# Running sums of a state-space scan: from additions on GpSimd to accumulating DMAs, with the closing of a segment spread over more pairs and the experts leading by 12

## The chip, the cores and the metric

The kernel runs on one core of a Trainium2 chip, as one program. The metric is the device time of one launch, in microseconds (us). The kernel before took 618.33 us (median of 3 runs, 615.45 to 619.60).

## The reference

Two layers work on x of shape (1, 2048, 128), each behind a modulated layer norm. The first has a decaying linear attention with a small feed-forward block, and then a mixture of 8 experts. The second has a selective state-space scan, and then a product in the frequency domain that is linear in its input. The change touches the scan and what follows it:

```python
# experts: hidden 512, the two best of 8 weigh the sum
h = gelu(einsum('te,ieh->tih', x, w1) + b1)
out = sum((einsum('tih,ihe->tie', h, w2) + b2) * weights[..., None], axis=1)
# scan over 2048 tokens: 256 channels, 16 states
dt = softplus(x[:, :, :64] @ W_dt.T + b_dt); Bm = x @ W_B.T; Cm = x @ W_C.T
dA = exp(dt_t[:, :, None] * A[None])
h = dA * h + (dt_t * xv_t)[:, :, None] * B_t[:, None, :]
y_t = einsum('bdn,bn->bd', h, C_t)          # the sum over the 16 states
y = (y * silu(z)) @ W_out.T
```

## The kernel before, in words

The tokens are cut into four segments of 512. The first 170 us or so hold the attention and its feed-forward block. After them comes one loop over "pairs of states": a pair p is two of the 16 states of a segment, so a segment has 8 pairs (NP) and there are 32 in all. The loop runs from p = -AHEAD to 31. In pass p every engine does its share of expert g = p + AHEAD (32 of them, 8 for each segment) and of pair p. With AHEAD = 13 the loop has 45 passes: 13 with an expert alone, 19 with an expert and a pair, 13 with a pair alone.

In one pass:

- PE: the expert's up products (L1204 to L1206, four quarters of three matmuls), its down products (L1216), and for each state one matmul that spreads the B row over all partitions into the bank pB (`row_b`, L1282).
- ACT: four GELUs (`hidden`, L958), then four exponentials `dA` for the next pair (`decays`, L970). It loads a table before either.
- DVE: for each state a product into PSUM (`products`, L733) and two scans (`scans`, L746, tile Hs, one half for each state of the pair), a small reduction of the last column (L750), and once a pass the sum of the expert's result into X (`moe_acc`, L717).
- POOL: for each state the product with the C row (`output`, L386), and, in the pairs below ALONE = 18, an addition to the segment's running sum (L392). The running sum lives in half of Zev. In the pairs from ALONE on, PE adds the products into the banks pY (`total`, L1298 and L1302).
- SP: loads the C rows of a pair, four pairs ahead (L327).

A table in `later_stages` puts the other work into passes, by the number k of the pair in its segment. An entry names a place in the pass: "A" and "B" stand on PE between the expert's products, "C" at its end, "mid" between the two states on DVE, "end" after them, "apply" at the end of ACT's pass. Closing a segment (its "tail") is: `gate` (the sum times silu(z), L490 on POOL or L757 on DVE), `project` (L1313 on PE, and L762 on DVE), the layer norm (`ln_stats`, `ln_apply`, `ln_turn`), `bias` (L456) and `fft` (L1321, L768). Preparing the next one (its "front") is: `ln_stats`, `ln_apply` (L820), `ln_turn` (L1014 and L834), and from k = 5 on the matmuls of `x_part` (L1257), `rows`, `dt_part` and `z_part`. On every engine the order of instructions is that of the program; semaphores make one engine wait for another.

## Time and profile before

| | us |
|---|---|
| median of 3 runs | 618.33 |
| the profiled execution | 618.62 |
| its span in the profile | 616.3 |
| PE busy | 494.2 (80%) |
| DVE busy | 429.7 (70%) |
| POOL busy | 373.5 (61%) |
| ACT busy | 360.7 (59%) |

The busy shares are means over stages that differ: no engine is busy all the time, and the shares alone don't say which of them sets the pace of a pass. The profiled execution took 2.3 us more than its span.

### The profile page before, as it was taken

To read this page: it belongs to the slowest core of one execution; us is meant where nothing else is said; L and a number is where in the kernel's file an instruction comes from. 1 tells how busy PE (TensorE), PEld (TensorE's weight loads), DVE (VectorE), ACT (ScalarE), POOL (GpSimd) and SP (SyncE) were. 2 spreads that over 40 slices of the span, in tenths; PEclk is the share of its full clock that TensorE was granted. 3 is DMA by queue.
4 is the path that set the end of the run, shared out by engine and by line. 5 is a ranking of instruction groups with operands and counts; after the bars stand their busy time and mean duration, and the time that the engine had idled before them with its cause. 6 is when DMAs were issued, how large, how long until landed. Compare 5 with 4: busy or idle time off the path is not lost.

```text
span 616.3 us, 6905 instructions
## 1 busy us (share of the span) xinstructions
PE 494.2 (80%) x2358; PEld 346.0 (56%) x2358; DVE 429.7 (70%) x723; ACT 360.7 (59%) x505; POOL 373.5 (61%) x234
## 2 busy tenths in 40 slices
PE   3878877679899999988879987969987678766663
PEld 3466555444678888667756766856766433233222
DVE  4757888964542441048997786988785996999961
ACT  0432442325675575689989985979985555734301
POOL 3225976847201111218999997999996767557541
PEclk9977998989999999999999988899988989889877
DMA  8600000000000000400202010112110112212000
GB/s 295 259 1 0 1 1 1 1 0 0 1 1 1 2 1 1 139 0 35 69 35 71 34 70 30 41 51 71 35 64 9 65 51 70 69 69 80 5 1 17
DMA packets 12562, 26.93 MB, mean 44 GB/s; under 512 B 1968, under 2 KB 7472, under 8 KB 12272
## 3 DMA queue, kind: packets, MB, share of 16 engines
q1 hardware_dynamic: 11952, 25.57, 11.9%
q10 hardware_dynamic: 576, 0.92, 0.4%
q8 instruction: 19, 0.31, 0.2%
q14 instruction: 15, 0.12, 0.1%
HBM read 25.31 MB, written 1.18 MB: 43 GB/s over the span
## 4 chain that ended last, share of the span: by engine, by line
DVE 34%; POOL 27%; PE 24%; issue 6%; ACT 6%; DMA 1%; ACTq 0%; POOLq 0%; DVEq 0%
POOL Zod L386 11%; POOL Zev L392 11%; DVE Hs L746 10%; DVE pCT L733 6%; PE pO L1216 5%; DVE S L641 5%; DVE pH L640 3%; PE pY L1076 1%; PE pY L1302 1%; PE pH L1204 1%; PE pH L1257 1%; ACT gel L958 1%; DMA S<-in_w_mod 1%; PE pY L1257 1%; PE pY L1313 1%
## 5 line engine op out<-in xcount | busy, mean ns | idle before, releaser
L1216 PEld LDWEIGHTS pO<-w_e,gel 128*128 128x128 f32 x1024 | 126.8, 198 | 17.9 <-issue 8.8
L1216 PE MATMUL pO<-w_e,gel 128*128 128x128 f32 x1024 | 129.0, 281 | 5.0 <-DVE X L717 4.7
L746 DVE TENSOR_TENSOR_SCAN Hs<-dA,HL,pCT 128x512 f32<-128x512 f32 x96 | 117.7, 1267 | 6.1 <-POOL Zod L386 4.5
L958 ACT ACTIVATE gel<-pH,b_e 128x512 f32<-128x512 f32 x128 | 86.0, 687 | 48.5 <-PE pH L1206 47.8
L970 ACT ACTIVATE dA<-dt,a_neg 128x512 f32<-128x512 f32 x128 | 81.9, 711 | 35.4 <-DVE Hs L746 35.2
L733 DVE TENSOR_TENSOR pCT<-u,pB 128x1024 f32<-128x1024 f32 x64 | 78.3, 1224 | 25.2 <-PE pB L1282 24.2
L386 POOL TENSOR_TENSOR Zod<-Hs,Crow 128x1024 f32<-128x1024 f32 x33 | 78.3, 2373 | 13.2 <-DVE Hs L746 11.6
L392 POOL TENSOR_TENSOR Zev<-Zev,Zod 128x1024 f32<-128x1024 f32 x33 | 79.9, 2422 | 2.6
L1204 PE MATMUL pH<-h2h,w_e1h 128*128 128x512 f32 x128 | 58.3, 456 | 20.4 <-ACT gel L958 19.1
L717 DVE SCALAR_TENSOR_TENSOR X<-pO,wts,X 128x128 f32<-128x128 f32 x128 | 35.8, 342 | 40.6 <-PE pO L1216 40.5
L386 POOL TENSOR_TENSOR Zev<-Hs,Crow 128x1024 f32<-128x1024 f32 x17 | 41.0, 2414 | 36.8 <-DVE Hs L746 33.3
L435 POOL TENSOR_TENSOR ZA<-Qsb,S 128x1024 f32<-128x1024 f32 x16 | 38.0, 2377 | 33.9 <-DVE S L641 32.6
L1282 PE MATMUL pB<-ST,sel 96*128 96x512 bf16 x64 | 25.7, 401 | 34.2 <-DVE pCT L733 34.0
L1206 PE MATMUL pH<-h2h,w_e1l 128*128 128x512 f32 x128 | 51.3, 401 | 0.0
L1205 PE MATMUL pH<-h2l,w_e1h 128*128 128x512 f32 x128 | 51.2, 400 | 0.0
L1204 PEld LDWEIGHTS pH<-h2h,w_e1h 128*128 128x128 f32 x128 | 24.2, 189 | 36.1 <-ACT gel L958 32.2
L386 POOL TENSOR_TENSOR ZS<-Hs,Crow 128x1024 f32<-128x1024 f32 x14 | 33.0, 2358 | 17.9 <-DVE Hs L746 17.9
L820 ACT ACTIVATE ln_x<-X,ln_nb,ln_rs 128x128 f32<-128x128 f32 x48 | 19.7, 481 | 34.2 <-POOL ln_nb L352 34.2
L746 DVE TENSOR_TENSOR_SCAN Hs<-dA,pCT 128x512 f32<-128x512 f32 x32 | 37.3, 1207 | 3.3 <-POOL Zod L386 2.6
L884 ACT COPY Qsb<-pCT 128x1024 f32<-128x1024 f32 x16 | 16.2, 1013 | 36.7 <-PE pCT L1092 36.7
L1282 PEld LDWEIGHTS pB<-ST,sel 96*128 96x128 bf16 x64 | 6.3, 98 | 53.0 <-DVE pCT L733 47.1
L1091 PE MATMUL pH<-qk_hi,pick 128*128 128x512 f32 x32 | 16.2, 507 | 22.2 <-DVE S L641 22.1
(223 smaller groups left out, 922.7 us busy)
## 6 DMA issues: line engine op xcount, KB each, us to landing
Crow<-c_rows SPq DMA_DIRECT2D x32, 512.0 KB, 3.7
w_e<-in_w_e SPq DMA_DIRECT2D x2, 2048.0 KB, 10.7
X<-in_x SPq DMA_DIRECT2D x4, 256.0 KB, 7.7
out<-h2T SPq DMA_DIRECT2D x4, 256.0 KB, 2.3
S<-in_w_mod ACTq DMA_DIRECT2D x2, 384.0 KB, 5.4
w_cx<-in_conv_row SPq DMA_DIRECT2D x1, 512.0 KB, 8.9
w_f<-in_w_f SPq DMA_DIRECT2D x2, 128.0 KB, 5.6
b_e<-in_b_e SPq DMA_DIRECT2D x1, 256.0 KB, 13.4
```

The source lines that it names most:

```text
L386: pool.tensor_tensor(Z, Hs[:, 2 * o:2 * o + 2, 0:w], Crow[:, 2 * (p % NCB) + o:2 * (p % NCB) + o + 1, 0:w].to_broadcast([P, ND, w]), ALU.m ...
L392: pool.tensor_tensor(acc_of(c), acc_of(c), Z, ALU.add).then_inc(s["mam_zs"], 1)
L435: pool.tensor_tensor(ZA[:, :, :], Qsb[:, 2 * (R % 2):2 * (R % 2) + 2, :], S[:, 2 * r:2 * r + 2, :], ALU.mult).then_inc(s["att_zo"], 1)
L717: ins = vec.scalar_tensor_tensor(Xj, pO[:, j * P:(j + 1) * P], wts[:, c, j * E + e:j * E + e + 1], Xj, ALU.mult, ALU.add)
L733: vec.tensor_tensor(pU[:, :, 0:w], half_of(u, c), pB[:, None, 0:w].to_broadcast([P, ND, w]), ALU.mult).then_inc(s["mam_ub"], 1)
L746: vec.tensor_tensor_scan(Hs[:, 2 * o + d, 0:w], dA[:, 4 * (p % 2) + 2 * o + d, 0:w], pU[:, d, 0:w], HL[:, d, n:n + 1] if c else 0.0, ALU.m ...
L958: nc.scalar.activation(gel[:, n % NG, 0:w], pH[n % 2][:, 0:w], ACT.Gelu_apprx_tanh, bias=b_e1[:, NK * e + k:NK * e + k + 1]).then_inc(s["m ...
L970: nc.scalar.activation(dA[:, 4 * (p % 2) + r, 0:WIDTHS[c]], half_of(dt, c)[:, r % 2, :], ACT.Exp, scale=a_neg[:, r % 2, n:n + 1]).then_inc ...
L1204: mm(pH[n % 2][:, 0:w], w_e1h[:, g % E, part], h2h[:, c, 0:w], start=True, stop=False)
L1205: mm(pH[n % 2][:, 0:w], w_e1h[:, g % E, part], h2l[:, c, 0:w], start=False, stop=False)
L1206: mm(pH[n % 2][:, 0:w], w_e1l[:, g % E, part], h2h[:, c, 0:w], start=False, stop=True).then_inc(s["moe_h"], 1)
L1216: ins = mm(pO[:, j * P:(j + 1) * P], gel[:, n % NG, j * P:(j + 1) * P], w_e2[:, NK * (g % E) + k, :], start=(k == 0 and j == 0), stop=(k = ...
```

## The change

There are four parts.

1. **Sums by DMA.** In pairs below ALONE the products of both states go to a whole tile (Zev for even pairs, ZS for odd ones), and one DMA issued by GpSimd adds that tile to `Acc` (128 x 2048 f32, 1 MB). The first pair of a segment writes its products straight into `Acc`. The additions of L392 go. Each DMA waits until the one before it has landed, and the products two pairs later wait for it too. `Acc` keeps the two states apart; `gate` adds its halves once.
2. **The closing is spread.** `gate` goes from the end of pass 0 to the middle of pass 1, `project` from 1 to 2, the sum into X and the statistics from the middle of pass 1 to the end of pass 2, `ln_turn` from place A of pass 3 to place C, with a tile h5T of its own.
3. **AHEAD = 12**, so ALONE = 20, and the loop has 12 passes with an expert alone, 20 with both, 12 with a pair alone.
4. **The preparation** starts (`ln_stats` of the front) in pass 4 and no longer in pass 3.

```diff
@@ -35,3 +35,3 @@
 NCB = 4
-AHEAD = 13
+AHEAD = 12
 HALO = TAPS - 1
@@ -160,3 +160,2 @@
         Zev = sb("Zev", [P, 2 * ND, TC])
-        Zod = sb("Zod", [P, ND, TC])
         ZS = sb("ZS", [P, 2 * ND, TC])
@@ -173,2 +172,4 @@
         HL = sb("HL", [P, ND, NS])
+        Acc = sb("Acc", [P, 2, 2 * ND, TC])
+        h5T = sb("h5T", [P, TC])
         outb = h2T[:, :].rearrange("p (j d) -> p j d", j=NJ)
@@ -213,2 +214,7 @@
 
+        def tail_bank(c):
+
+            return [(stage_bank(p, at)) for p, stages in later_stages() for at, stage, q, *_ in stages
+                    if stage == "project" and q == c][0]
+
         def totals(p):
@@ -221,10 +227,5 @@
 
-        def adds(m):
-
-            return m - m // NS
+        def sums(p):
 
-        def acc_of(c):
-
-            h = ND * ((c + 1) % 2)
-            return Zev[:, h:h + ND, 0:WIDTHS[c]]
+            return len([q for q in range(min(p + 1, ALONE)) if q % 2 == p % 2 and q % NP])
 
@@ -247,2 +248,3 @@
         mam_c = [sem(f"mam_c{i}") for i in range(NCB)]
+        mam_s = [sem(f"mam_s{i}") for i in range(2)]
         NSM, NAT, NFF, NMO, NMA = 6, 2, 2, 5, 10
@@ -263,7 +265,7 @@
                 if 0 <= tail:
-                    plan += [(0, "end", "gate", tail), (1, "A", "project", tail), (1, "mid", "ln_stats", tail),
-                             (2, "apply", "ln_apply", tail), (2, "end", "bias", tail), (3, "A", "ln_turn", tail, 2),
-                             (4, "A", "fft", tail)]
+                    plan += [(1, "mid", "gate", tail), (2, "A", "project", tail), (2, "end", "tail_x", tail),
+                             (2, "end", "ln_stats", tail), (3, "apply", "ln_apply", tail), (3, "C", "ln_turn", tail, 2),
+                             (3, "end", "bias", tail), (4, "A", "fft", tail)]
                 if 0 <= front < NL:
-                    plan += [(3, "mid", "ln_stats", front), (4, "apply", "ln_apply", front), (4, "C", "ln_turn", front, 1),
+                    plan += [(4, "mid", "ln_stats", front), (4, "apply", "ln_apply", front), (4, "C", "ln_turn", front, 1),
                              (5, "A", "x_part", front, 0), (5, "B", "rows", front), (6, "A", "x_part", front, 1),
@@ -281,4 +283,5 @@
             last = NL - 1
-            for stage in (("A", "total", NL * NP - 1), ("end", "gate", last), ("A", "project", last), ("end", "bias", last),
-                          ("mid", "ln_stats", last), ("apply", "ln_apply", last), ("A", "ln_turn", last, 2), ("A", "fft", last)):
+            for stage in (("A", "total", NL * NP - 1), ("end", "gate", last), ("A", "project", last), ("end", "tail_x", last),
+                          ("end", "bias", last), ("mid", "ln_stats", last), ("apply", "ln_apply", last),
+                          ("A", "ln_turn", last, 2), ("A", "fft", last)):
                 yield (NL * NP, [stage])
@@ -365,3 +368,3 @@
                 h = slice(2 * (p % 2), 2 * (p % 2) + 2)
-                first = k == 0 and o == 0
+                part = slice(2 * o, 2 * o + 2)
                 if alone(p):
@@ -370,8 +373,7 @@
                         pool.wait_ge(s["mam_y"], totals(p - 2))
-                    elif o == 0 and p % 2 == (c + 1) % 2:
-                        pool.wait_ge(s["mam_y"], 1)
-                    elif o == 0:
-                        pool.wait_ge(s["mam_y2"], 2 * c)
-                elif first:
-                    Z = acc_of(c)
+                    elif p == ALONE and o == 0:
+                        for q in (p - 2, p - 1):
+                            pool.wait_ge(mam_s[q % 2], 16 * sums(q))
+                elif k == 0:
+                    Z = Acc[:, c % 2, part, 0:w]
                     if c >= 2:
@@ -379,5 +381,5 @@
                 else:
-                    Z = Zod[:, :, 0:w]
-                    if adds(m - 1):
-                        pool.wait_ge(s["mam_zs"], adds(m - 1))
+                    Z = [Zev, ZS][p % 2][:, part, 0:w]
+                    if p >= 2 and o == 0 and sums(p - 2):
+                        pool.wait_ge(mam_s[p % 2], 16 * sums(p - 2))
                 if o == 0:
@@ -389,6 +391,13 @@
                 done["mam_z"] = m + 1
-                if not alone(p) and not first:
-                    pool.wait_ge(s["mam_z"], m + 1)
-                    pool.tensor_tensor(acc_of(c), acc_of(c), Z, ALU.add).then_inc(s["mam_zs"], 1)
-                    done["mam_zs"] = adds(m)
+
+            def add_up(p):
+
+                c, k = divmod(p, NP)
+                if alone(p) or k == 0:
+                    return
+                w = WIDTHS[c]
+                pool.wait_ge(s["mam_z"], 2 * p + 2)
+                if sums(p - 1):
+                    pool.wait_ge(mam_s[(p - 1) % 2], 16 * sums(p - 1))
+                pool.dma_start(Acc[:, c % 2, :, 0:w], [Zev, ZS][p % 2][:, :, 0:w], accum_op=ALU.add).then_inc(mam_s[p % 2], 16)
 
@@ -484,3 +493,4 @@
                     return
-                pool.wait_ge(s["mam_zs"], adds(NS * (c + 1) - 1))
+                w, p = WIDTHS[c], NP * (c + 1) - 1
+                pool.wait_ge(mam_s[p % 2], 16 * sums(p))
                 pool.wait_ge(s["mam_gz"], ND * (c + 1))
@@ -488,4 +498,8 @@
                     pool.wait_ge(s["mam_o"], c)
+                pool.tensor_tensor(Acc[:, c % 2, 0:2, 0:w], Acc[:, c % 2, 0:2, 0:w], Acc[:, c % 2, 2:4, 0:w],
+                                   ALU.add).then_inc(s["mam_zs"], 1)
+                pool.wait_ge(s["mam_zs"], c + 1)
+                done["mam_zs"] = c + 1
                 for d in range(ND):
-                    pool.tensor_tensor(y2[:, d, 0:WIDTHS[c]], acc_of(c)[:, d, :], half_of(gz, c)[:, d, :],
+                    pool.tensor_tensor(y2[:, d, 0:w], Acc[:, c % 2, d, 0:w], half_of(gz, c)[:, d, :],
                                        ALU.mult).then_inc(s["mam_y2"], 1)
@@ -493,2 +507,8 @@
 
+            def run(stages, last):
+
+                for at, stage, c, *k in stages:
+                    if (at in ("B", "C", "end")) == last and stage in ("ln_stats", "rows", "route", "gate", "bias"):
+                        {"ln_stats": ln, "rows": rows, "route": route, "gate": gate, "bias": bias}[stage](c)
+
             for p, stages in later_stages():
@@ -496,6 +516,7 @@
                     output(p, 0)
+                run(stages, False)
+                if 0 <= p < NL * NP:
                     output(p, 1)
-                for at, stage, c, *k in stages:
-                    if stage in ("ln_stats", "rows", "route", "gate", "bias"):
-                        {"ln_stats": ln, "rows": rows, "route": route, "gate": gate, "bias": bias}[stage](c)
+                    add_up(p)
+                run(stages, True)
 
@@ -758,6 +779,6 @@
 
-            def project(c, b):
+            def tail_x(c):
                 vec.wait_ge(s["mam_o"], c + 1)
                 Xc = rows_of(X, c)
-                sig(vec.tensor_tensor(Xc, Xc, tokens(PS[b], c), ALU.add), "mam_x", c + 1)
+                sig(vec.tensor_tensor(Xc, Xc, tokens(PS[tail_bank(c)], c), ALU.add), "mam_x", c + 1)
 
@@ -776,6 +797,6 @@
                         continue
-                    if stage in ("ln_stats", "step", "gate"):
-                        {"ln_stats": ln_stats, "step": step, "gate": gate}[stage](c)
-                    elif stage in ("route", "weigh", "project", "fft"):
-                        {"route": route, "weigh": weigh, "project": project, "fft": fft}[stage](c, b)
+                    if stage in ("ln_stats", "step", "gate", "tail_x"):
+                        {"ln_stats": ln_stats, "step": step, "gate": gate, "tail_x": tail_x}[stage](c)
+                    elif stage in ("route", "weigh", "fft"):
+                        {"route": route, "weigh": weigh, "fft": fft}[stage](c, b)
 
@@ -974,3 +995,3 @@
 
-                ln([h2T, h4T, h4T][which][:, 0:WIDTHS[c]], c, 2 + 2 * which, b, None if which else h2h[:, c, 0:WIDTHS[c]])
+                ln([h2T, h4T, h5T][which][:, 0:WIDTHS[c]], c, 2 + 2 * which, b, None if which else h2h[:, c, 0:WIDTHS[c]])
 
@@ -1295,5 +1316,7 @@
                 if p == ALONE and k:
-                    pe.wait_ge(s["mam_zs"], adds(2 * p - 1))
+                    for q in (p - 2, p - 1):
+                        pe.wait_ge(mam_s[q % 2], 16 * sums(q))
                     for d in range(ND):
-                        mm(pY[d][:, 0:w], ident[:, :], acc_of(c)[:, d, :], start=True, stop=False)
+                        for o in range(2):
+                            mm(pY[d][:, 0:w], ident[:, :], Acc[:, c % 2, 2 * o + d, 0:w], start=(o == 0), stop=False)
                 for o, Z in ((0, Zev), (1, ZS)):
@@ -1320,3 +1343,3 @@
                 for j in range(blocks(c)):
-                    ins = mm(PS[b][:, j * P:(j + 1) * P], h4T[:, j * P:(j + 1) * P], w_fft[:, :], start=True, stop=True)
+                    ins = mm(PS[b][:, j * P:(j + 1) * P], h5T[:, j * P:(j + 1) * P], w_fft[:, :], start=True, stop=True)
                 ins.then_inc(s["fft_o"], 1)
@@ -1398,3 +1421,3 @@
     arrays = {n: np.ascontiguousarray(x) for n, x in arrays.items()}
-    nc = bacc.Bacc("TRN2", target_bir_lowering=False, num_devices=1)
+    nc = bacc.Bacc("TRN2", target_bir_lowering=False, num_devices=1, dynamic_dma_scratch_size=2048)
     aps = {n: nc.dram_tensor(f"in_{n}", x.shape, mybir.dt.from_np(x.dtype), kind="ExternalInput").ap()
```

POOL, where the first segment ends and the second begins. Of the kernel before, from the last product of pair 7 to the first addition of pair 9:

```order
L386 TENSOR_TENSOR Zod<-Hs,Crow 128x1024
L392 TENSOR_TENSOR Zev<-Zev,Zod 128x1024
L386 TENSOR_TENSOR Zev<-Hs,Crow 128x1024
L386 TENSOR_TENSOR Zod<-Hs,Crow 128x1024
L392 TENSOR_TENSOR Zev<-Zev,Zod 128x1024
L490 TENSOR_TENSOR y<-Zev,gz 128x512 x2
L386 TENSOR_TENSOR Zod<-Hs,Crow 128x1024
L392 TENSOR_TENSOR Zev<-Zev,Zod 128x1024
```

Of the change, the same place, from the products of pair 7 to the DMA of pair 9:

```order
L388 TENSOR_TENSOR ZS<-Hs,Crow 128x1024 x2
L402 DMA Acc<-ZS 128x2048
L388 TENSOR_TENSOR Acc<-Hs,Crow 128x1024 x2
L388 TENSOR_TENSOR ZS<-Hs,Crow 128x1024
L499 TENSOR_TENSOR Acc<-Acc 128x1024
L504 TENSOR_TENSOR y<-Acc,gz 128x512 x2
L388 TENSOR_TENSOR ZS<-Hs,Crow 128x1024
L402 DMA Acc<-ZS 128x2048
```

The additions after the products are gone, a DMA stands once a pair, and the gate stands between the two products of pair 9.

DVE, pairs 9 and 10. Of the kernel before, from the scans of pair 9's first state (the projected rows go into X at L762):

```order
L746 SCALAR_TENSOR_TENSOR Hs<-dA,HL,pCT 128x512 x2
L750 TENSOR_REDUCE HL<-Hs 128x2
L717 SCALAR_TENSOR_TENSOR X<-pO,wts,X 128x128 x4
L762 TENSOR_TENSOR X<-X,pY 128x512
L523 BN_STATS ln_st<-X 128x6 x4
L526 BN_AGGR ln_mv<-ln_st 128x2 x4
L733 TENSOR_TENSOR pCT<-u,pB 128x1024
```

Of the change, from the scans of pair 10's second state:

```order
L754 TENSOR_TENSOR pCT<-u,pB 128x1024
L767 SCALAR_TENSOR_TENSOR Hs<-dA,HL,pCT 128x512 x2
L771 TENSOR_REDUCE HL<-Hs 128x2
L783 TENSOR_TENSOR X<-X,pY 128x512
L544 BN_STATS ln_st<-X 128x6 x4
L547 BN_AGGR ln_mv<-ln_st 128x2 x4
L754 TENSOR_TENSOR pCT<-u,pB 128x1024
```

The sum into X, and the statistics behind it, stand a pair and a half later.

PE, in pass 21 of the change (k = 5 of the third segment), the first one after the last running sum:

```order
L1278 MATMUL pH<-h3T,w_cx 128x512 x4
L1321 MATMUL pY<-Acc,ident 128x512 x4
L1325 MATMUL pY<-Zev,ident 128x512 x2
L1325 MATMUL pY<-ZS,ident 128x512 x2
L1284 MATMUL pH<-h3T,w_bc 96x512
```

The running sum enters the banks pY by four matmuls here, right behind an `x_part`. In the kernel before it entered by two (L1298) in pass 19, two passes ahead of that `x_part`.

## Rows read from the trace of the kernel before

**Rows 1.** The page, part 1: busy us (share), instructions of each engine.

```profile
PE 494.2 (80%) x2358; PEld 346.0 (56%) x2358; DVE 429.7 (70%) x723; ACT 360.7 (59%) x505; POOL 373.5 (61%) x234
```

**Rows 2.** The page, part 5: costliest groups, busy and mean ns, idle before.

```profile
L386 POOL TENSOR_TENSOR Zod<-Hs,Crow 128x1024 f32<-128x1024 f32 x33 | 78.3, 2373 | 13.2 <-DVE Hs L746 11.6
L392 POOL TENSOR_TENSOR Zev<-Zev,Zod 128x1024 f32<-128x1024 f32 x33 | 79.9, 2422 | 2.6
```

**Rows 3.** What ACT waited for, 282 to 354 us: total, times, longest.

```profile
ACT gel L958 <- PE pH L1206: 3.3, 7, 0.5
```

**Rows 4.** Timeline of ACT, table loads before GELUs: start, us, what.

```profile
292.62 1.28 ACT L958 ACT_TABLE_LOAD   x1
300.94 1.28 ACT L958 ACT_TABLE_LOAD   x1
...
309.26 1.28 ACT L958 ACT_TABLE_LOAD   x1
...
320.71 1.28 ACT L958 ACT_TABLE_LOAD   x1
...
332.15 1.28 ACT L958 ACT_TABLE_LOAD   x1
...
345.53 1.28 ACT L958 ACT_TABLE_LOAD   x1
...
356.24 1.28 ACT L958 ACT_TABLE_LOAD   x1
...
448.74 1.28 ACT L958 ACT_TABLE_LOAD   x1
```

**Rows 5.** Timeline of DVE, products that open pairs 10, 11, 16 and 24.

```profile
380.40 1.22 DVE L733 TENSOR_TENSOR pCT<-u,pB 128x1024 f32<-128x1024 f32 x1
...
389.18 1.22 DVE L733 TENSOR_TENSOR pCT<-u,pB 128x1024 f32<-128x1024 f32 x1
...
446.77 1.22 DVE L733 TENSOR_TENSOR pCT<-u,pB 128x1024 f32<-128x1024 f32 x1
...
530.95 1.22 DVE L733 TENSOR_TENSOR pCT<-u,pB 128x1024 f32<-128x1024 f32 x1
```

**Rows 6.** Timeline of all engines where segments 0 and 1 are closed.

```profile
371.64 2.92 PE L1313 MATMUL pY<-w_out,y 128*128 128x128 f32 x16 [2.70 <-POOL y L490]
...
374.67 0.69 DVE L762 TENSOR_TENSOR X<-X,pY 128x512 f32<-128x512 f32 x1 [6.17 <-PE pY L1313]
...
376.59 1.21 DVE L733 TENSOR_TENSOR pCT<-u,pB 128x1024 f32<-128x1024 f32 x1
...
409.89 1.65 ACT L820 ACTIVATE ln_x<-X,ln_nb,ln_rs 128x128 f32<-128x128 f32 x4 [2.09 <-POOL ln_nb L352]
...
468.22 0.69 DVE L762 TENSOR_TENSOR X<-X,pY 128x512 f32<-128x512 f32 x1 [7.18 <-PE pY L1313]
```

**Rows 7.** Timeline of PE, first up products of experts 8, 9 and 10.

```profile
226.14 0.48 PE L1204 MATMUL pH<-h2h,w_e1h 128*128 128x512 f32 x1
...
234.19 0.48 PE L1204 MATMUL pH<-h2h,w_e1h 128*128 128x512 f32 x1
...
241.35 0.48 PE L1204 MATMUL pH<-h2h,w_e1h 128*128 128x512 f32 x1
```

**Rows 8.** Timeline of PE and DVE, pass 21.

```profile
507.67 1.88 PE L1302 MATMUL pY<-Zev,ident 128*128 128x512 f32 x4
...
511.11 1.02 PE L1263 MATMUL pH<-h3T,w_bc 128*96 128x512 f32 x2
...
512.38 1.23 DVE L733 TENSOR_TENSOR pCT<-u,pB 128x1024 f32<-128x1024 f32 x1 [3.61 <-PE pB L1282]
```

**Rows 9.** DMA: queue (packets, MB, share of 16 engines), issues (KB, us to landing).

```profile
q1 hardware_dynamic: 11952, 25.57, 11.9%
...
Crow<-c_rows SPq DMA_DIRECT2D x32, 512.0 KB, 3.7
w_e<-in_w_e SPq DMA_DIRECT2D x2, 2048.0 KB, 10.7
```

## The prediction, as it stood before the changed kernel ran

> **What bounds the kernel now.** I read the busy shares first. PE leads with 80%, DVE has 70%, POOL 61%, ACT 59% [rows 1]; that decides nothing, since the stages differ. So I took the loop segment by segment and asked who waits.
>
> POOL works four times a pair in the pairs with a running sum: two products of 2.37 us and two additions of 2.42 us [rows 2], 9.6 us or so. It has the largest share of the late chain, and the change relieves it. But in segment 0 it isn't the bound. From 282 to 354 us ACT waited 3.3 us in all for PE's up products [rows 3], so it was busy nearly throughout. Its passes, from one table load before the GELUs to the next, take 8.32 us (300.94 to 309.26) where nothing is added, then 11.45 in pass 4 (layer norm of the front), 11.44 in 5, 13.38 in 6, 10.71 in 7 [rows 4]. Those are ACT's own instructions. POOL falls behind at 9.6 against 8.3 and catches up in the long passes.
>
> In segment 1 (356.24 to 448.74, 92.5 us on ACT [rows 4]) POOL's lag comes out. The gate waits for the last addition, `project` waits 2.70 us for the gate, and DVE waits 6.17 us for `project`, in the middle of pass 9; in pass 17 that wait is 7.18 us. ACT later waits 2.09 us for the layer norm's POOL part, which stands behind additions [rows 6]. The least that a pass takes once a previous state enters the scans is DVE's 8.78 us (380.40 to 389.18 [rows 5]). PE is the bound where pairs run alone beside an `x_part`: in pass 21 DVE waited 3.61 us for it [rows 8].
>
> **The change, part by part.**
>
> *Lead of 12.* One pass with an expert alone goes. It is pass 9 of the experts, 7.16 us (234.19 to 241.35), while pass 8 (8.05 us, 226.14 to 234.19) [rows 7] now also holds the front's layer norm: four transposes and a wait for ACT, about 1.0 us by what pass 9 has over its 6.7 us of plain work (an estimate from that pass's own length). Gain 6.2 us. One pass moves from "pair alone" to "both"; that is counted in segment 2.
>
> *Segment 0.* Same passes on ACT, 80.2 us as now. The statistics in pass 4 come one pass later, but the layer norm starts behind ACT's exponentials in either version, and on POOL it now stands between two products with no additions ahead. Gain 0.
>
> *Segment 1.* Pass by pass, us: 9.0 (k = 0, as now), 8.8 (DVE), 10.7 in pass 10 (DVE's 8.8 and the 1.9 of X and statistics, 374.67 to 376.59 [rows 6]; PE with `project` has about as much), 11.5 in pass 11 (the tail's `ln_turn` at "C" costs ACT what the front's costs in pass 4 [rows 4]), 11.5, 11.4, 13.4, 10.7. Sum 87.0 against 92.5: gain 5.5. The 6.17 and 2.09 us go; 3 us are given back in pass 11, where a transpose at "C" makes PE wait for ACT.
>
> *Segment 2* (446.77 to 530.95, 84.2 us [rows 5]). Passes 16 to 18 as above (9.2, 8.8, 10.7), pass 19, now with an expert, 9.5 on DVE, since ACT's extra work there delays nothing behind it. Pass 20: 7.7 of pair, 1.25 of statistics, 0.7 of `fft`: 9.6. Pass 21 took 11.3 us, 3.6 of it waiting for PE [rows 8]. Its `total` lasts 3.44 us (507.67 to 511.11 [rows 8]) for four matmuls; four more for the running sum make it 14.8. Passes 22 and 23 as now, 9.7 and 8.9. Sum 81.2: gain 3.0.
>
> *Segment 3 and the end.* DVE has no gap there and the same work. Gain 0.
>
> *The gate* on POOL, one addition of 2.4 and two products of 1.25, stands between two products of pair 9: the second ends some 10 us after the scans of pair 9's first state, when DVE needs its half of Hs at 11. POOL has lost its 4.8 us of additions, which is its cover. If that cover fails, DVE stalls by the difference.
>
> *17 DMAs on GpSimd*, 7 + 7 + 3. No row shows an accumulating DMA or one issued by GpSimd. What it moves, 1.05 MB, is bounded by the plain copies: queue q1 moved 25.57 MB in 11.9% of 616.3 us = 73.3 us, 0.349 MB/us, and a C row load of 0.52 MB landed after 3.7 us [rows 9], 1.5 of data and 2.2 fixed. So 5.2 us if only the written bytes count, 8.2 if source and destination are both read at that rate, 11.2 if three transfers follow one another. I take 8.2: an addition needs both, and reads and writes of one copy overlap already. A pair lasts 8.3 us or more, so it fits, barely. The DMA holds POOL itself only while it is issued; between 0.3 and 3.8 us would hide in the room between two products (4.75) and a pass (8.5). In pass 20 the first product waits for pair 19's DMA: up to 3 us on DVE, hidden behind PE's pass 21.
>
> The Trainium skill, page "DMA: Bandwidth & Descriptors", section "Anatomy of one DMA — SWDGE (gpsimd) path", gives 2.0 us and the bytes over 436 GB/s for a DMA of GpSimd, which would be 4.4 us here (an estimate by that page). By that price the sum comes out the same, with room to spare; nothing in it speaks of accumulation.
>
> Sum: 6.2 + 0 + 5.5 + 3.0 = 14.7. The profiled execution took 618.62 us, 2.3 over its span and 0.3 over the median, so both bases agree: **604 us**.
>
> **Rivals.**
>
> *A, the DMA is too slow.* Each DMA waits for its predecessor on POOL, in front of the next products; so a pair can't be shorter than the landing time and some 0.5 us. Half of Hs is needed again 6.4 us after its scan and the product takes 2.4, so 4 us of lag are free in each segment. With a landing of 11.2 (11.7 a pair) segment 0 needs 82 us for seven pairs, against 72 + 4: +6; segment 1, 82 against 78 + 4: none; segment 2, 35 against 29 + 4: +2; 612 us. With 11.5 it is 617, so from about 11.6 on nothing is gained. If three MB each took what one takes of the 2 MB load (10.7 / 2 [rows 9]), it would be 16 us: 115.5 a segment, +39, +33, +17: 693 us. For it: two reads and a write of a whole MB. Against: plain copies of twice the size land in 10.7 us.
>
> *B, POOL stays occupied.* If issuing costs POOL as much as the two additions did, 4.8 us, a pair remains at 9.6 on POOL. The lead and the new order of the closing remain: 6.2, about 3 in segment 1 and 1 in segment 2: 608 to 610 us. For it: no row shows the price of issuing. Against: SP's rows for issuing are short, but SP isn't POOL. The Trainium skill, same page, section "SWDGE vs HWDGE vs iDMA", says that software on GpSimd computes each descriptor, which is the mechanism of this rival; no run here shows its time yet.
>
> *C, the preparation is tighter than I think.* Statistics, POOL, ACT, PE and the matmuls behind them stand within one pass now. If each of the three fronts and two tails stalls ACT by another 1.5 us, 7.5 of the gain go: 611.5 us. For it: ACT waited 2.09 us for POOL in this very chain. Against: the additions that delayed POOL are gone.
>
> **How the numbers follow.** Two runs of this kernel differ by up to 4 us; I take 1%, 6.2 us, as what can be told from no change, so "faster" ends at 612. Forecast 0.58 (its own range 597 to 609), B 0.12, C 0.12, A near no change (612 to 624) 0.06, A beyond 624 0.12. Forecast, B and half of C are faster: 0.76. The other half of C and the first part of A are the same: 0.12. Slower: 0.12. The range for 8 in 10 is 595 to 620: below 604 by what my pass lengths may overstate (3 us a segment), above it to take in B, C and the landing of 11.2 to 11.5.
>
> **What the profile after would show.** Step 1: the first product of pair 0 at about 266 us, not 272. Step 2: segment 0 on ACT again at 80 us. Step 3: no wait of DVE for `project` in pass 10 (or 18), segment 1 at 87. Step 4: pass 21 near 15 us, with PE as the one that DVE waits for. Step 5: landing times of the sum near 8 us, and POOL waiting for DVE, not DVE for POOL. Wrong would be: landings above 9 us with POOL's products starting right at them (A), gaps on POOL behind each DMA with the products late (B), ACT's `ln_x` waiting for POOL or PE's first `x_part` for ACT (C).

## The result, and the profile after

The changed kernel took 614.91 us (median; 612.5 to 619.68), the kernel before 619.39 beside it: a ratio of 0.9938 (95% interval 0.9913 to 0.9963). The gain is 0.6%, 4.5 us of median, where I had forecast 14.7. It is within the 1% that I had set as no change. The profiled execution took 613.03 us, its span 611.0 against 616.3, so 5.3 us are there to be found.

The page's part 1, the answer to [rows 1]: GpSimd (POOL) has lost 59 us of work, and TensorE (PE) 14, with 12 matmul records fewer; VectorE (DVE) and ScalarE (ACT) have what they had within 3 us.

```profile
PE 480.0 (79%) x2346; PEld 335.5 (55%) x2346; DVE 430.9 (71%) x723; ACT 363.4 (59%) x507; POOL 314.4 (51%) x220
```

I took the time apart at DVE's products that open the pairs, as [rows 5] does, from both traces (us; forecast of the change in the last column):

| stretch | before | after | change | forecast |
|---|---|---|---|---|
| to the first product of pair 0 | 271.95 | 263.57 | -8.4 | -6.2 |
| segment 0 | 81.8 | 80.3 | -1.5 | 0 |
| segment 1 | 93.0 | 85.5 | -7.5 | -5.5 |
| segment 2 | 84.2 | 92.6 | **+8.4** | -3.0 |
| segment 3, to its last product | 60.1 | 63.7 | **+3.6** | 0 |
| from there to the end | 25.3 | 25.3 | 0 | 0 |

The first three terms brought 17.4 us, more than the forecast wanted from all. Two stretches gave 12.0 back. In segment 2 it is one pass: passes 16 to 23 took 11.1, 8.8, 10.7, 8.8, 10.8, **23.8**, 9.7, 8.9. The timeline of pass 20 and 21 in the changed kernel, where [rows 8] stood before (in brackets: idle time ahead, and what ended it):

```profile
471.56 0.94 POOL L402 DMA_DIRECT2D Acc<-ZS  x1 [0.30 <-POOL ZS L388]
...
477.07 2.45 DVE L767 TENSOR_TENSOR_SCAN Hs<-dA,HL,pCT 128x512 f32<-128x512 f32 x2
...
480.73 2.34 POOL L388 TENSOR_TENSOR Zev<-Hs,Crow 128x1024 f32<-128x1024 f32 x1 [6.92 <-DMA Acc<-ZS]
...
483.20 2.45 DVE L767 TENSOR_TENSOR_SCAN Hs<-dA,HL,pCT 128x512 f32<-128x512 f32 x2 [2.36 <-POOL Zev L388]
...
484.90 0.20 POOL L355 TENSOR_TENSOR ln_nb<-ln_nm,ln_rs 128x4 f32<-128x4 f32 x1
...
485.13 1.65 ACT L841 ACTIVATE ln_x<-X,ln_nb,ln_rs 128x128 f32<-128x128 f32 x4 [11.88 <-POOL ln_nb L355]
...
486.93 1.08 PE L1035 MATMUL pH<-ident,ln_x 128*128 128x128 f32 x4 [9.23 <-ACT ln_x L841]
...
488.97 6.50 PE L1278 MATMUL pH<-h3T,w_cx 128*128 128x512 f32 x8 [0.53 <-ACT h3T L855]
...
495.31 3.59 PE L1321 MATMUL pY<-Acc,ident 128*128 128x512 f32 x8
498.74 1.88 PE L1325 MATMUL pY<-Zev,ident 128*128 128x512 f32 x4
500.46 1.88 PE L1325 MATMUL pY<-ZS,ident 128*128 128x512 f32 x4
502.17 1.02 PE L1284 MATMUL pH<-h3T,w_bc 128*96 128x512 f32 x2
503.04 0.38 PE L1303 MATMUL pB<-ST,sel 96*128 96x512 bf16 x1
...
503.45 1.23 DVE L754 TENSOR_TENSOR pCT<-u,pB 128x1024 f32<-128x1024 f32 x1 [11.07 <-PE pB L1303]
```

Read it from the bottom: DVE idles 11.07 us for row B, which stands on PE behind `x_part`, the sums and `rows`. These wait for the turned rows, these for `ln_x`, which idled ACT 11.88 us for `ln_nb`. And `ln_nb`, the last of four small operations on 4 columns that finish the statistics, is late since it is queued on POOL behind pair 20's first product, which waited 6.92 us for pair 19's DMA: issued at 471.56, landed 9.1 us later. The windows add a second thing: the granted clock (PEclk) when `x_part` ran.

```profile
480.00:488.00 8.00, 1.07 (x5) 0.85 (x5) 3.45 (x4) 1.65 (x4) 6.96 (x7) 0.50 0.03 8
488.00:496.00 8.00, 7.47 (x12) 3.09 (x11) 3.84 (x4) 5.00 (x7) 4.05 (x2) 0.58 0.00 0
496.00:504.00 8.00, 7.41 (x18) 2.89 (x16) 0.55 (x1) 0.93 (x3) 0.00 (x0) 1.00 0.00 0
```

Columns: window, us, then busy us of PE, PEld, DVE, ACT, POOL, the clock, DMA share, GB/s. PE had worked 1.07 us of 8 and was at 0.50, the lower of its levels (1.2 of 2.4 GHz).

In segment 3 the loss is in pass 25, where DVE now makes segment 2's gate in the middle of the pass:

```profile
533.26 1.29 DVE L778 TENSOR_TENSOR y<-pY,gz 128x512 f32<-128x512 f32 x2
...
534.61 3.78 PE L1325 MATMUL pY<-Zev,ident 128*128 128x512 f32 x4 [3.41 <-DVE y L778]
...
538.18 2.31 PE L1325 MATMUL pY<-ZS,ident 128*128 128x512 f32 x4
...
540.82 1.23 DVE L754 TENSOR_TENSOR pCT<-u,pB 128x1024 f32<-128x1024 f32 x1 [2.64 <-PE pB L1303]
```

The sums of pair 24 reuse the banks that the gate reads, so PE waits for it, runs them at a lowered clock (0.50 from 534 to 538 us), and DVE then waits for the row B behind them.

### The profile page after: what moved, and what is told of

The parts are those of the page before. It is cut to its first block, busy times and chain, and to the rows that moved or that the text cites. A ratio compares the mean times of both kernels' runs of the same rounds, so it can differ in the third digit from the quotient of the medians.

```text
span 611.0 us, 6868 instructions
## 1 busy us (share of the span) xinstructions
PE 480.0 (79%) x2346; PEld 335.5 (55%) x2346; DVE 430.9 (71%) x723; ACT 363.4 (59%) x507; POOL 314.4 (51%) x220
## 3 DMA queue, kind: packets, MB, share of 16 engines
q0 software_dynamic: 2448, 17.83, 14.4%
## 4 chain that ended last, share of the span: by engine, by line
PE 18%; ACT 15%; DVE 13%; issue 7%; POOL 5%; DMA 3%; POOLq 0%; ACTq 0%; DVEq 0%
DVE Hs L767 7%; DVE pCT L754 4%; ACT dA L991 4%; PE pO L1237 3%; ACT gel L979 3%; DMA Acc<-ZS 3%; ACT L991 3%; PE pY L1325 2%; PE pY L1278 2%; POOL ZS L388 2%; PE pH L1225 2%; ACT L979 2%; PE pH L1278 2%; ACT ln_x L841 2%; PE pH L1227 1%
## 5 line engine op out<-in xcount | busy, mean ns | idle before, releaser
L1237 PEld LDWEIGHTS pO<-w_e,gel 128*128 128x128 f32 x1024 | 125.5, 196 | 17.4 <-issue 8.8
L388 POOL TENSOR_TENSOR ZS<-Hs,Crow 128x1024 f32<-128x1024 f32 x32 | 75.9, 2376 | 51.0 <-DVE Hs L767 51.0
L388 POOL TENSOR_TENSOR Zev<-Hs,Crow 128x1024 f32<-128x1024 f32 x26 | 63.7, 2452 | 28.6 <-DVE Hs L767 21.4
L905 ACT COPY Qsb<-pCT 128x1024 f32<-128x1024 f32 x16 | 16.2, 1013 | 37.1 <-PE pCT L1113 37.1
L662 DVE TENSOR_TENSOR_SCAN S<-cols,S,pH 128x512 f32<-128x512 f32 x24 | 30.7, 1280 | 0.9
```

The source lines that it names most:

```text
L388: pool.tensor_tensor(Z, Hs[:, 2 * o:2 * o + 2, 0:w], Crow[:, 2 * (p % NCB) + o:2 * (p % NCB) + o + 1, 0:w].to_broadcast([P, ND, w]), ALU.m ...
L1237: ins = mm(pO[:, j * P:(j + 1) * P], gel[:, n % NG, j * P:(j + 1) * P], w_e2[:, NK * (g % E) + k, :], start=(k == 0 and j == 0), stop=(k = ...
```

## The experiments

Each was timed in five rounds beside the kernel before. For segments 2 and 3 the steadiest measure is the profiled time from pair 16's first product to the last one: 144.3 us before, **156.3** after. It is one execution of each kernel. The kernel before was timed anew beside each batch (medians 618.4 to 620.83), so kernels are compared by their ratios and not by their medians.

| kernel | median us | ratio to before (95%) | that stretch | pass 21 |
|---|---|---|---|---|
| changed kernel | 614.91 | 0.9938 (0.9913-0.9963) | 156.3 | 23.8 |
| e1, late wait | 607.47 | 0.9802 (0.9757-0.9847) | 149.3 | 16.7 |
| e11, statistics first | 607.19 | 0.9793 (0.9770-0.9817) | 149.1 | 16.7 |
| e2, gate back | 613.25 | 0.9889 (0.9857-0.9920) | 153.0 | 23.9 |
| e3, e1 and e2 | 605.34 | 0.9759 (0.9714-0.9804) | 144.6 | 16.9 |
| e4, e3 and sum in pass 24 | 604.60 | 0.9758 (0.9714-0.9802) | 144.1 | 13.5 |
| e10, e4 and row B first | 604.44 | 0.9746 (0.9716-0.9775) | 144.2 | 8.7 |
| e9, e4 and PE kept busy | 602.45 | 0.9711 (0.9676-0.9745) | 141.1 | 10.2 |
| e7, e3 without DMAs | 604.24 | 0.9776 (0.9743-0.9808) | 145.5 | 16.7 |
| e12, DMAs alone | 612.67 | 0.9878 (0.9854-0.9901) | 145.2 | 9.7 |
| e6, lead of 13 | 614.34 | 0.9937 (0.9905-0.9968) | 148.6 | 12.7 |
| e8, all but the DMAs | 618.33 | 1.0007 (0.9979-1.0035) | 149.6 | 14.1 |
| e5, lead and preparation | 637.36 | 1.0326 (1.0297-1.0355) | 154.7 | 20.4 |

**e1, the wait of pair 20.**

```diff
-                    elif p == ALONE and o == 0:
-                        for q in (p - 2, p - 1):
-                            pool.wait_ge(mam_s[q % 2], 16 * sums(q))
+                    elif p == ALONE:
+                        pool.wait_ge(mam_s[o], 16 * sums(p - 2 + o))
```

> Only the wait of pair 20 is changed: its first product on GpSimd waits for pair 18's DMA (whose tile it overwrites), its second product alone for pair 19's. Theory (the stall of pass 21 comes from pair 19's DMA, landed 480.7 in the changed kernel, ahead of which GpSimd held the first product, and behind that product the statistics of segment 3's normalisation): the first product starts right behind the issue at about 471.7, ln_nb is there at about 476.3, ScalarE's ln_x ends at 478, the transposes at 479.2, x_part runs 480 to 483.6, the sums behind it to 490.5, rows to 491.4, and VectorE's first product of pass 22 stands at about 491.6 instead of 503.45: 11.8 us less, near 601 to 603 us where the changed kernel has 613 to 615. Rival 1 (the clock is low in pass 20 whatever the wait is, since TensorE has no experts there): x_part still takes 6.5 instead of 3.6 us, 8 to 9 us less, 605. Rival 2 (pass 21 is bound by TensorE's own work, x_part, eight sums and rows, and the wait is hidden by it): within 2 us of the changed kernel, 613.

Pass 21 fell from 23.8 to 16.7 us and no other pass moved by more than 0.1: the wait is worth 7.1 us. The theory had said 11.8, since it gave `x_part` 3.6 us. The trace of e1:

```profile
473.62 2.62 POOL L387 TENSOR_TENSOR Zev<-Hs,Crow 128x1024 f32<-128x1024 f32 x1
...
478.06 0.20 POOL L355 TENSOR_TENSOR ln_nb<-ln_nm,ln_rs 128x4 f32<-128x4 f32 x1
...
482.13 6.38 PE L1277 MATMUL pH<-h3T,w_cx 128*128 128x512 f32 x8 [0.49 <-ACT h3T L854]
...
496.50 1.23 DVE L753 TENSOR_TENSOR pCT<-u,pB 128x1024 f32<-128x1024 f32 x1 [9.03 <-PE pB L1302]
```

`ln_nb` comes at 478.06 instead of 484.90 (the statistics reach POOL only at 476.3, not at 474 as I had assumed), and `x_part` still takes 6.38 us. So rival 1 was right about the clock, the theory about the wait.

**e11, the same wait, but the statistics ahead of the product.**

```diff
+                if p == ALONE:
+                    run(stages, False)
                 if 0 <= p < NL * NP:
                     output(p, 0)
-                run(stages, False)
+                if p != ALONE:
+                    run(stages, False)
```

> The changed kernel with its wait of pair 20's first product for both DMAs kept, and with one move on GpSimd: in pass 20 the statistics of segment 3's normalisation stand ahead of that product instead of behind it. Theory (what made pass 21 long is not the product but the statistics queued behind it, since ln_x, its transposes, x_part and then row B follow from them): pass 21 takes 16.7 us as with the later wait, not 23.8, the whole 7 us less, 607 to 608. Rival (the late product itself holds the sums of pair 20 and VectorE's scans, which wait for the tile): pass 21 takes 20 us or more, 611 or more.

16.7 us to the tenth, as in e1. The product started as late as before, when the DMA had landed:

```profile
482.17 2.35 POOL L388 TENSOR_TENSOR Zev<-Hs,Crow 128x1024 f32<-128x1024 f32 x1 [2.62 <-DMA Acc<-ZS]
```

So what made pass 21 long is the four small operations queued behind the product.

**e2, the gate at the end of pass 24.**

```diff
-                    plan += [(1, "mid", "gate", tail), (2, "A", "project", tail), (2, "end", "tail_x", tail),
+                    plan += [(1, "mid", "gate", tail) if summed(tail) else (0, "end", "gate", tail), (2, "A", "project", tail), (2, "end", "tail_x", tail),
```

> Only the place of the gate that VectorE makes for segment 2 is changed: at the end of pass 24 as before the change, instead of the middle of pass 25. Theory (the 3.41 us that TensorE waits for the gate in front of pair 24's sums, then 2.64 us of VectorE waiting for row B, are segment 3's 3.7 us): segment 3 on VectorE takes 64 us again instead of 67.5, the whole 3 to 4 us less. Rival (at the end of pass 24 the gate waits for the sums of pair 23 instead, and VectorE stalls for as long there): within 1 us of the changed kernel.

Passes 24 and 25 took 8.7 and 7.5 instead of 7.5 and 11.3, pass 29 7.5 instead of 8.2; the stretch fell by 3.3 us. The intervals of the two ratios overlap a little (0.9857-0.9920 and 0.9913-0.9963), so it is the profile that shows the size. PE no longer waits for the gate, but for VectorE's and GpSimd's products of its own pair:

```profile
530.45 1.29 DVE L778 TENSOR_TENSOR y<-pY,gz 128x512 f32<-128x512 f32 x2
...
532.93 0.39 PE L1303 MATMUL pB<-ST,sel 96*128 96x512 bf16 x1 [4.56 <-POOL ZS L388]
...
533.15 3.56 PE L1325 MATMUL pY<-Zev,ident 128*128 128x512 f32 x4
```

**e3, both**, and **e4**, which also moves the identity matmuls:

> Both edits, the later wait of pair 20 and the gate at the end of pass 24. Theory (two separate stalls, one in segment 2 and one in segment 3): they add, 11.8 + 3.7 = 15.5 us less than the changed kernel, 598 to 601 us. Rival (the first stall gone, TensorE comes into pass 24 late with its sums and the gate stalls there for what it saves): no more than the first edit alone, 602.

```diff
-                if p == ALONE and k:
+                if p == NP * (ALONE // NP + 1) - 1 and ALONE % NP:
...
-                            mm(pY[d][:, 0:w], ident[:, :], Acc[:, c % 2, 2 * o + d, 0:w], start=(o == 0), stop=False)
+                            mm(pY[d][:, 0:w], ident[:, :], Acc[:, c % 2, 2 * o + d, 0:w], start=False, stop=False)
...
-                        ins = mm(pY[d][:, 0:w], ident[:, :], Z[:, h + d, 0:w], start=(k == 0 and o == 0),
+                        ins = mm(pY[d][:, 0:w], ident[:, :], Z[:, h + d, 0:w], start=((k == 0 or p == ALONE) and o == 0),
```

> Both edits, and the four identity matmuls that bring the running sum from SBUF into PSUM stand in pass 24 ahead of pair 23's sums instead of pass 21 ahead of pair 20's. Theory (pass 21 is TensorE's once the wait is gone: x_part 3.4, sum 3.4, pair 20's sums 3.4, rows 0.9 ahead of row B): another 3.4 us less than with both edits, 595 to 597 us. Rival (what bounds pass 24 is the same engine: the gate waits for pair 23's sums, which end 3.4 us later): the same as with both edits, 598 to 601.

In e3 the two gains add, though the 605.34 us lie above both ranges that I had given, since these went by the 11.8: 11.7 us are off the stretch, of which 7.1 + 3.3 are theirs and 1.6 a shorter pass 16 in that execution (a matter of the clock, shown further down). In e4 pass 21 lost 3.4 us as the theory said; passes 24 and 26 took 1.2 and 0.3 more. Pass 16, which the edit doesn't touch, took 11.1 us against 9.5 in e3's profile, so the stretch ended only 0.5 us shorter. The medians can't tell e4 from e3, and both of its ranges were missed from above for the same reason; by the passes some 2 us of the 3.4 stay.

**e10, row B ahead of the sums**, on e4:

```diff
+                early = ALONE < p < NP * (ALONE // NP + 1)
+                if early:
+                    row_b(2 * p + 2)
                 if 0 < p < NL * NP:
                     total(p - 1)
...
-                if 0 <= 2 * p + 2 < NL * NS:
+                if 0 <= 2 * p + 2 < NL * NS and not early:
```

> The kernel with both edits and the running sum brought in at pass 24, with row B of the next pair ahead of the sums of the pair before on TensorE in passes 21 to 23 (it stood behind them). Theory (VectorE idles 5.8 us in pass 21 for a row B that needs nothing of what stands ahead of it; with it ahead of the sums, 3.4 us, and the rows, 0.9 us, these run beside VectorE): pass 21 takes 9.1 instead of 13.5 us, passes 22 and 23 take 8.3 and 9 to 10, so 4 to 5 us less, about 600 us against 604.6. Rival (TensorE's own work, 26 us of the 36 from 468 to 504, sets the end of pass 23, and what pass 21 gains passes 22 and 23 give back): within 1 us, 604.

Passes 21 to 24 took 8.7, 8.3, 12.3, 12.3 against 13.5, 9.7, 8.9, 9.9: 41.7 against 42.0. The rival holds: the order of PE's work only moves VectorE's gap. That PE's own work from `ln_x` of the last preparation on sets when this stretch ends is what remains, and e9 agrees with it.

**e9, PE kept busy in pass 20**, on e4:

```diff
+                if p == ALONE:
+                    pe.wait_ge(s["ln_evac"], L[0])
+                    warm(pY0, 5)
...
                 if 0 <= 2 * p + 2 < NL * NS:
                     row_b(2 * p + 2)
+                if p == ALONE:
+                    warm(pY0, 2)
```

> The kernel with both edits and the running sum brought in at pass 24, with seven 512-column identity matmuls more in pass 20 on TensorE, whose results are overwritten: five before row B of pair 21 and two behind it, in time that the engine spent idle (4.9 and 2.3 us). Theory (x_part of pass 21 takes 6.6 us since the granted clock was 0.50 from 480 to 488 behind idle time; eight such matmuls take 3.4 at a clock of 1.00): the clock is near 1.0 in pass 21, x_part takes 3.4 to 3.6 us, pass 21 takes 10.4 instead of 13.5, and the kernel 3 us less, 601 to 602 us against 604.6. Rival 1 (the clock is low in that stretch whatever the engine does): x_part at 6.5 and no change, 604.6. Rival 2 (VectorE's idle in pass 21 is for ln_x, not for x_part's length): no change in pass 21 though x_part is shorter.

The first line is of e4, the others are of e9:

```profile
484.89 6.62 PE L1277 MATMUL pH<-h3T,w_cx 128*128 128x512 f32 x8 [0.49 <-ACT h3T L854]
...
475.70 4.46 PE L1067 MATMUL pY<-X,ident 128*128 128x512 f32 x10
...
485.39 3.67 PE L1282 MATMUL pH<-h3T,w_cx 128*128 128x512 f32 x8 [0.26 <-ACT h3T L854]
...
493.61 1.23 DVE L753 TENSOR_TENSOR pCT<-u,pB 128x1024 f32<-128x1024 f32 x1 [2.44 <-PE pB L1307]
```

Its windows, in the columns above:

```profile
480.00:488.00 8.00, 5.89 (x17) 2.54 (x17) 7.86 (x9) 5.16 (x10) 4.76 (x6) 1.00 0.46 105
488.00:496.00 8.00, 6.68 (x18) 2.75 (x17) 5.46 (x6) 4.23 (x6) 5.23 (x4) 1.00 0.02 4
```

The clock stayed at 1.00, `x_part` took 3.67 us instead of 6.62, pass 21 took 10.2 instead of 13.5, and the stretch is 3.0 us shorter, as the theory said (each 512-column matmul is two records, so the expectation's eight are four matmuls). One pair of profiles could be luck, but in the ten other profiles with a lead of 12 this `x_part` took 5.47 to 6.62 us. This is the fastest version: 2.9% below the kernel before, with an interval wholly below the changed kernel's. Against e4 the two intervals overlap; there the profile decides, not the medians.

**e7, no DMAs at all**, on e3: `pool.dma_start(Acc...)` becomes `pool.sem_inc(mam_s[p % 2], 16)`. It leaves out what the DMAs add, and keeps every wait.

> The kernel with both edits (the later wait of pair 20, the gate at the end of pass 24), with the 17 accumulating DMAs left out; their semaphores are counted up by GpSimd instead. The running sums of three segments lack all pairs but the first and those alone, so the output is not the reference's. Theory (with pair 20's wait gone all DMAs are hidden behind a pass or more, and their issue, 0.9 us of GpSimd each, lies in idle time): within 2 us of the kernel with both edits, 603 to 605 us, its passes each within 0.3 us but for pass 21, which starts the sums no earlier. Rival (the DMAs slow other engines: GpSimd's product behind an issue took 2.65 instead of 2.37 us, and GpSimd waits for up to 3.3 us ahead of some): passes 9, 12 and 16, which took 11.3, 12.5 and 11.1 us, fall by 1 to 3 us each, 598 to 600.

Every pass is within 0.3 us of e3's (pass 21 took 16.7 against 16.9) but for pass 16, 11.1 against 9.5. Once pair 20 no longer waits, 17 DMAs of 1 MB cost nothing that shows; the ratios' intervals overlap.

**The parts by themselves.** e5 is the kernel before with `AHEAD = 12` and the front's statistics at pass 4. e6 is the changed kernel with `AHEAD = 13`. e8 is the changed kernel's order with GpSimd's additions, and with e2's place of the gate. e12 is the changed kernel with the lead, the preparation and the closing of before.

> The kernel before with a lead of 12 and the preparation's statistics in pass 4 of a segment (at pass 3 the rows of X are not final with this lead); GpSimd's additions, the closing's places and its tiles stay. Theory (the lead is worth the 8.3 us that the changed kernel's first product came earlier, less the 1 to 2 us that one more pair of states costs beside an expert; the rest of the change gives 7.5 us in segment 1 and loses 8.4 + 3.7 in segments 2 and 3): the first product near 263.6, 612 to 613 us, no slower than the whole change. Rival (with a lead of 12 GpSimd's additions of pairs 18 and 19 and the tail's waits of 12 and 9 us cost more, so that only with the other parts does the lead pay): 616 or more.

> The changed kernel with a lead of 13 again: running sums by DMA, spread closing and the preparation in pass 4, with pairs 18 and 19 alone and so two DMAs less in segment 2. Theory (the stall of pass 21 is made by the lead: pair 20's first product stands behind pair 19's DMA only since 20 is the first alone pair; here that pair is 18 and no preparation hangs on it, the statistics come two passes later): the first product at 272, segment 1 at 85.5, segment 2 at 84 to 86, segment 3 at 67, so 619.4 - 1.5 - 7.5 + 0 to 2 + 3.5 = 614 to 616 us. Rival (the stall is in the DMA sums with any lead): segment 2 at 92, 622 us.

> All of the change but the DMAs: GpSimd adds each product to the running sum itself, as before, with a lead of 12, the spread closing, the preparation in pass 4, the gate of segment 2 at the end of pass 24 and no wait of pair 20 for a DMA. Theory (GpSimd at 92% busy in segment 1 is what made the tail late; with its additions kept the closing still waits for it, and what the DMAs bring is the difference): segment 1 at 88 to 91 us instead of 85.5, 608 to 612 us, slower than the kernel with both edits at 605. Rival (the spread alone takes the wait off VectorE, and GpSimd's additions end within the pass anyway): segment 1 at 85 to 86, and 603 to 606.

> The DMAs alone: the running sums by accumulating DMA and what belongs to them (two tiles, GpSimd's order, the tile of the closing's turned rows), with a lead of 13, the preparation in pass 3 and the closing at its places of before (gate at the end of pass 0, project in pass 1, and so on). Theory (GpSimd's busy time was what made gate and projection late, 6.2 and 7.2 us of waiting on VectorE in passes 9 and 17; the last DMA of a segment lands 9 us behind its issue, nearly a pass, so about half of the two waits stays): first product at 272, 609 to 613 us. Rival 1 (the DMA and the gate's own addition behind it are as late as the additions were; the spread is what removes the waits): 617 to 620. Rival 2 (both waits vanish, and the spread only costs): 605 or less.

e5 fell on its rival's side, and further out: 3.3% **slower**. Passes 5, 13 and 21 took 22.4, 22.6 and 20.4 us. Pass 5 in its trace:

```profile
317.11 2.34 POOL L392 TENSOR_TENSOR Zev<-Zev,Zod 128x1024 f32<-128x1024 f32 x1
319.53 0.24 POOL L349 TENSOR_SCALAR ln_nm<-ln_mv 128x4 f32<-128x4 f32 x1
...
321.26 0.20 POOL L352 TENSOR_TENSOR ln_nb<-ln_nm,ln_rs 128x4 f32<-128x4 f32 x1
...
321.49 1.65 ACT L820 ACTIVATE ln_x<-X,ln_nb,ln_rs 128x128 f32<-128x128 f32 x4 [9.18 <-POOL ln_nb L352]
...
327.44 1.23 DVE L733 TENSOR_TENSOR pCT<-u,pB 128x1024 f32<-128x1024 f32 x1 [10.63 <-PE pB L1282]
```

It is pass 21 of the changed kernel once more: the statistics stand on POOL behind products and additions, and ACT, PE and DVE wait in turn. e8, whose statistics stand between two products, is better but has passes 5, 12 and 20 at 18.0, 16.2 and 16.1 us, and in the end it is as fast as the kernel before. Against e3 (0.9759) the DMAs are worth 2.5% there; without them no kernel with a lead of 12 came out ahead of the kernel before. The lead of 12 alone on the DMAs, and the spread closing alone on GpSimd's additions, were not run. My theory for e8 had the slowness in segment 1 alone (90.2 us, in its range) and missed segment 0 (85.5) and 2 (88.9).

e12, the DMAs alone, came as forecast, and is faster than the whole change. Segments 1 and 2 took 86.9 and 83.7 us; the gate still waits for the last DMA, but DVE's wait for `project` is 2.63 us, where [rows 6] had 6.17, and 3.97 where it had 7.18:

```profile
364.77 2.38 POOL L499 TENSOR_TENSOR Acc<-Acc 128x1024 f32<-128x1024 f32 x1 [0.58 <-DMA Acc<-ZS]
...
371.96 0.69 DVE L783 TENSOR_TENSOR X<-X,pY 128x512 f32<-128x512 f32 x1 [2.63 <-PE pY L1336]
```

e12 has the stall of the first alone pair too: pair 18's first product waited 7.67 us for pair 17's DMA, and pass 19 took 13.9 us where the kernel before took 10.0. It differs from e6 only in the closing's places and the start of the preparation, and e6 is no faster for them (0.9937, 0.9905 to 0.9968): the spread gained 1.4 us in segment 1 and lost 2.6 in segment 2. So beside the DMAs and with a lead of 13 the later places do not pay.

e6 took what I expected, but not for the reason. The stall of the first alone pair is there with a lead of 13 too (pass 19 took 14.9 us); only the preparation isn't behind it, and of POOL's wait of 9.37 us DVE sees 6.06:

```profile
474.34 2.33 POOL L388 TENSOR_TENSOR Zev<-Hs,Crow 128x1024 f32<-128x1024 f32 x1 [9.37 <-DMA Acc<-ZS]
...
476.80 2.45 DVE L767 TENSOR_TENSOR_SCAN Hs<-dA,HL,pCT 128x512 f32<-128x512 f32 x2 [6.06 <-POOL Zev L388]
```

## Why the prediction was wrong, by its steps

The direction was right and the size was not: the sum said 14.7 us, the runs gave 4.5.

**Lead of 12 (forecast 6.2): right.** The pair of profiles shows 8.4, but the start of pair 0 differs between executions of the same code. In the eleven profiles with a lead of 12 it came at 263.6 to 267.6, 265.5 on average; in the three with 13 at 271.6 to 273.1, 272.2 on average. That is 6.8. So 1.6 of the pair's 5.3 us are luck of the execution. The term itself was a little low by its own working: pass 9's 7.16 us are 0.5 over the 6.7 of plain work, not the 1.0 that I took off, and with 0.5 it would have been 6.7.

**Segments 0 and 1 (0 and 5.5): right in mechanism, gains of 1.5 and 7.5.** ACT's passes in segment 0 took 80.2 us again, as forecast. No wait of DVE for `project` is left in pass 10 or 18. Segment 1 took 85.3 us on ACT where I had summed 87.0; ACT's wait for POOL's statistics fell from 2.09 [rows 6] to 0.52 us.

**The 17 DMAs: right in the time, in part by luck.** The page of the changed kernel:

```profile
q0 software_dynamic: 2448, 17.83, 14.4%
...
Crow<-c_rows SPq DMA_DIRECT2D x32, 512.0 KB, 4.0
Acc<-ZS POOLq DMA_DIRECT2D x10, 1024.0 KB, 8.7
Acc<-Zev POOLq DMA_DIRECT2D x7, 1024.0 KB, 7.0
```

They landed after 7.0 to 9.8 us, median 8.6, where the sum took 8.2 from source and destination both moved at q1's rate: 6.0 us of data and 2.2 fixed. The page counts the bytes once (17.83 MB are one MB a DMA). Its packets took 14.4% of 611.0 us, 5.2 us a DMA, which is 1.7 times q1's time for a MB and not twice; that leaves 3.4 us of the 8.6 for the rest. So the two parts missed in opposite directions, and what the second transfer costs isn't shown. POOL was held 0.9 us by each issue. The Trainium skill's formula (page "DMA: Bandwidth & Descriptors", "Anatomy of one DMA — SWDGE (gpsimd) path"), which gave 4.4 us, does not agree with these rows. In e7 no cost of theirs elsewhere shows.

**"In pass 20 the first product waits for pair 19's DMA: up to 3 us on DVE, hidden behind PE's pass 21": the step that failed.** I had the wait and its length on DVE (2.36 us). I did not ask what stands behind the waiting product on POOL: `ln_nm`, `ln_ve`, `ln_rs`, `ln_nb`, from which PE's pass 21 itself starts. So PE's pass could not hide the wait; it was moved by it. Pass 21 took 23.8 us against my 14.8, and of the 9.0 between them 7.1 are the wait (e1, e11). The running sum's four matmuls cost the 3.4 that I gave them (e4). The clock, which I had not looked at, gives 1.4: `x_part` took 6.50 us, and in the kernel before, whose pass I carried over, it took 5.09, the next one 3.60:

```profile
502.74 5.09 PE L1257 MATMUL pH<-h3T,w_cx 128*128 128x512 f32 x8
...
513.90 3.60 PE L1257 MATMUL pH<-h3T,w_cx 128*128 128x512 f32 x8
```

So the clock was low there before the change too (0.79 from 500 to 504 us, 0.78 from 504 to 508), and of the 3.0 to 3.4 us that e9 gains some 1.5 were to be had without it by these rows (no run kept PE busy in the kernel before). The last 0.5 us of the 9.0 are not accounted for.

The rest of segment 2 missed by 2.4 (pass 16 +1.9, pass 20 +1.2, pass 19 -0.7). Of pass 16's 1.9 the clock is 1.6. The expert's down products in it, first in the changed kernel, then in e3, whose pass 16 took 9.5 us:

```profile
436.74 3.53 PE L1237 MATMUL pO<-w_e,gel 128*128 128x128 f32 x16
...
440.98 1.95 PE L1236 MATMUL pO<-w_e,gel 128*128 128x128 f32 x16
```

The clock was 0.50 from 436.7 to 438.4 us and 0.54 to 440.2 in the changed kernel, and 1.00 throughout in e3; DVE waited 2.27 us for the row B behind it against 0.65.

**"Segment 3 and the end. Gain 0": failed by 3.3 us** (e2). I looked for gaps on DVE, found none, and took the gate's new place as free. But segment 2's gate is on DVE, and pair 24's sums on PE wait for it, since they start anew in the banks that it reads.

**The rivals.** A fell: the DMAs stayed below its 11.6 us, and without them (e7) no pass was more than 0.3 us shorter than in the other profiles of this order. B fell: an issue held POOL for 0.9 us and not for 4.8. (The 59 us less of busy time can't tell, since issues don't count as busy.) C comes nearest in what it says would be seen (`ln_x` waiting for POOL, `x_part` for ACT), but it had 1.5 us in five places, and it was one wait of 11.88 us on ACT, worth 7.1, in the one pass where a DMA stands ahead of the statistics.

The two misses and what was repaid: 7.1 + 3.3 + 3.0 of clock are 13.4 us, and a kernel without them (e9) stands 18 us below the kernel before, past the 14.7 of the forecast; but half of the 3.0 of clock is no loss of the change. What stays open is why the clock fell in pass 16 of the changed kernel and not of e3, where PE had done the same work in the 8 us ahead of these products (6.1 us of it in either), and why it was 0.70 from 316 to 324 us in e9's profile, where pass 5, ahead of the edit's place, took 14.9 us instead of 12.6.

## What to carry to other kernels

For each wait that a change adds, list what is queued behind the waiting instruction on its engine, down to the smallest; an operation on 4 columns that starts the next stage costs the whole wait, while the big operation ahead of it may cost nothing. Put such small operations ahead of the first instruction that can wait for a transfer, and split a wait so that each tile waits only for its own last reader. When a consumer is moved, look for who overwrites what it reads, on every engine: that reader's place is the place where the next writer stalls.

## What the runs showed of the hardware

- A DMA that adds 1 MB from SBUF into SBUF landed after 7.0 to 9.8 us in the changed kernel (6.9 to 10.1 over all profiles), and 17 of them (14.4% of the DMA engines' span) lengthened nothing that shows in the passes beside them (e7); the C rows' DMAs landed after 4.0 instead of 3.7 us.
- GpSimd is held 0.9 us by each issue. Five of its products in the changed kernel took 2.65 to 2.68 us instead of 2.35, and none did where the DMAs were left out (e7).
- From 468 to 480 us TensorE worked 3.8 us in the changed kernel, 6.2 in e4 and 10.3 in e9. From 480 to 488 it was granted 0.50 (1.2 GHz), 0.50 and 1.00 (2.4 GHz), and the four 512-column matmuls of `x_part` took 6.50, 6.62 and 3.67 us. Matmuls without use, in idle time, were worth 3 us.
- The granted clock differed between executions behind the same work: in pass 16 sixteen records of down products took 3.53 us in one profile and 1.95 in another.
